# One graph layer on one core: gate logits out of the node products, expert weights asked for earlier, one-hot tiles scaled on ScalarE

## The chip, the core and the metric

The kernel runs on one core of a Trainium2 chip. The metric is the device time of one execution in microseconds, as the median of several runs. A core has five engines that run their own instruction lists: TensorE (matrix products, PE in the profile, with its weight loads as PEld), VectorE (DVE), ScalarE (ACT), GpSimd (POOL) and SyncE (SP), which here only issues DMAs. They wait for each other through semaphores (`wait_ge`, `then_inc`). All instructions of this kernel are written by hand in order, engine by engine; nothing is planned or reordered later.

## The reference

```python
xn = _layernorm(x)                                   # 3125 nodes, 256 features
gate = sigmoid(silu(rbf @ W1 + b1) @ W2 + b2)        # 50000 edges
aggr = segment_sum(gate * xn[src], dst)
x = x + xn + (silu(concat[xn, aggr] @ U1 + c1) @ U2 + c2) + mix(xn)
# mix: per head, k and v layer-normed, kv = k^T v / S, then (q kv) @ wo.T + bo
z = _layernorm(x)
logits = z @ gate_w + gate_b                          # 16 experts
top_probs, top_idx = top_k(softmax(logits), 2)        # renormalised to sum 1
x = x + sum over the two experts of p * ((silu(z @ w1[e]) * (z @ w2[e])) @ w3[e])
```

## The kernel before, in words

The nodes lie in 25 tiles of 128 rows (`NT`), two tiles to an iteration `v` of the node loop (13 iterations, `NB`). The kernel has four stages.

*Setup.* For each tile t, VectorE makes the normed rows, TensorE transposes them and projects them to k and v (`project`), and nine tiles later adds their k^T v sum (`sum_kv`, KLAG = 9). ScalarE copies and squares, VectorE sums the squares (`sum_sq`), makes the scales in batches (`kv_seed`, `kv_step`) and scales k (`scale_k`). SP stores the normed rows tile by tile and loads two parameters behind each store. Behind it the k^T v matrix is folded with `wo` and `wq` into one 256x256 matrix M (`mix_kv`, `mix_a1`, `mix_m`), between the first edge groups.

*Edges.* 98 groups of 512 edges: two products with silu and tanh, gathered source rows multiplied in, and a product with a one-hot matrix that sums messages into windows of `agg`.

*Nodes.* In iteration v TensorE runs `node_u1(v+1)` (24 products of 256 columns), `node_m(v+1)` (12 products, xn with M) and `node_silu(v)` (12 products, silu output with U2), the last two into the same PSUM bank. Operands are split in a high and a low half, so each logical product is three. VectorE adds the bank to x (`x1`), takes statistics, and at the ends of `CHUNKS` makes `rstd` and `nmr`. ScalarE writes the normed rows (`xn2`), SP stores them to `xn2_d`. For the gate logits TensorE transposes the normed rows (`transpose_xn2`, L1509), ScalarE copies them (`copy_xt2`, L807), TensorE multiplies by `gw` (`gate_logits`, L1682) and ScalarE copies the logits (`copy_lg`, L811); `XN2AT` says in which iteration a tile's rows are made. The last five tiles are done behind the loop.

*Routing and experts.* VectorE picks the top two experts (`top`, `top2`), counts them per expert (`count`, with two triangular-sum products on TensorE), turns counts into ranks (`picked`, `ranks`) and, when the count of all tiles is known, into places. The table slot -> node is a product of one-hot matrices: `low_marks(c)` makes one-hots over 128 positions, `high_marks(c)` one-hots over 80 blocks of 128 slots, once times the tile number and once times the row code; four batches (`TCUT`), two of these three factors on VectorE and the row one on ScalarE (the last batch wholly on VectorE). `place(c)` multiplies on TensorE. VectorE reads the table (L1423 to L1425), GpSimd gathers the slot rows together with their two gate weights (`gather_slots`), for which `wts` has been written by one DMA into two extra columns of `xn2_d` (L456). SP loads each expert block's weights (`load_w`), whose expert number it reads from `texp`; that is made behind the last marks (L1413 to L1418). Then comes the expert loop with blocks of 256 slots: `turn` (transposes), `expert_up`, `expert_down`, and GpSimd's scatter with accumulation to the output.

Each queue keeps its order: SP's is xn2 stores, output stores, the `wts` store, then all expert weights; GpSimd's first gather waits for the xn2 stores, for the `wts` store, for the table (`s_tabi`) and for `s_wsl`.

Of the kernel before, what the change touches and what calls it, by code (L numbers as in the profile page):

```python
# [23 lines left out]
i32 = mybir.dt.int32  # L24
# [4 lines left out]
P = 128  # L29
# [16 lines left out]
HC = HF // P  # L46
SB = 256
CHUNKS = ((0, 6), (6, 12), (12, 16), (16, 20), (20, NT))
NB = -(-NT // 2)
XN2AT = {3: (0, 2), 4: (2, 4), 5: (4, 6), 6: (6, 8), 7: (8, 10), 8: (10, 12), 9: (12, 14), 10: (14, 18), 11: (18, 20)}  # L50
RCUT = (0, 6, 12, NT)
XN2B = 4
TCUT = (0, 6, 12, 18, NT)
NTC = len(TCUT) - 1
TAILB = (6, 7, 0, 1)
RBANK = (2, 3, 4)
# [49 lines left out]
def gps_layer(nc, x_d, src_d, dst_d, first_d, rbf_d, W1_d, b1_d, W2_d, b2_d, U1_d, c1_d, U2_d, c2_d,  # L106
              wq_d, wkvT_d, woT_d, bo_d, kg_d, kb_d, vg_d, vb_d, gw_d, gb_d, w1_d, w2_d, w3_d, out_d):
# [6 lines left out]
    with ctx:  # L114
# [22 lines left out]
        U2 = sb("U2", [P, DC, D])  # L137
# [20 lines left out]
        M = wkv[:, :, 0:D]  # L158

# [3 lines left out]
        def part(mem, at, *shape):  # L163
# [4 lines left out]
            if len(shape) == 3:  # L168
# [19 lines left out]
        UMs = [part(fr, 8704 + 1024 * k, 2 * DC, D) for k in range(2)]  # L188
        xns = [[part(fr, 512 * (2 * i + k), DC, 2 * P) for k in range(2)] for i in range(2)]
        ags = [[part(fr, 2048 + 512 * (2 * i + k), DC, 2 * P) for k in range(2)] for i in range(2)]  # L190
        sts = [[part(fr, (4096, 10752)[i] + 512 * k, DC, 2 * P) for k in range(2)] for i in range(2)]
# [22 lines left out]
        xt2 = [oflat[i % 2][:, i // 2 * D:(i // 2 + 1) * D].rearrange("p (c q) -> p c q", c=DC) for i in range(4)]  # L214
# [15 lines left out]
        me, cu = ([part(big, EV + 2000 + 448 * k + NX * (a + r), NX, b - a + 1)  # L230
                   for r, (a, b) in enumerate(zip(RCUT, RCUT[1:]))] for k in range(2))
        mask = [part(big, EV + 2896 + 112 * min(r, 1) * 1, NX, b - a + 1)
                for r, (a, b) in enumerate(((0, 6), (12, NT)))]
        t_a = part(big, EV + 3232, 8, NX)
        tcmp = part(big, EV + 3360, CAPB, NX)
# [14 lines left out]
              for (mem, at), a, b in zip(((flat3(U1), 0), (flat3(h1f), 0), (flat3(wkv), 0), (big, EV + 4608)),  # L250
                                         TCUT, TCUT[1:])]
        tE = [marks(mem, at, (b - a) * NS).rearrange("p (n w) -> p n w", w=NS)
              for (mem, at), a, b in zip(((rbf[0], 0), (rbf[1], 0), (big, EV + 5728)), TCUT, TCUT[1:])]
        c_i = sb("c_i", [P, NX], i32)
        texp = sb("texp", [P, CAPB], i32)
        lastp = sb("lastp", [P, 1], i32)
# [83 lines left out]
        s_tp2 = sem("xn2_transposed")  # L340
        s_xt2 = sem("xt2_copied")
        s_lg = sem("logits_done")
        s_lgc = sem("logits_copied")
# [39 lines left out]
        NPAR = 21  # L383
# [3 lines left out]
        def _(sp):  # L387
# [4 lines left out]
            for k, (a, b) in enumerate(zip(XCUT, XCUT[1:])):  # L392
# [10 lines left out]
                (U2[:, :, :], U2_d.rearrange("(c p) n -> p c n", p=P)),  # L403
# [9 lines left out]
                (gw[:, :, :], gw_d.rearrange("(c p) n -> p c n", p=P)), (gb[:, :], row(gb_d, NX)),  # L413
# [41 lines left out]
            sp.wait_ge(s_wt, 1)  # L455
            sp.dma_start(xn2_d[:, D:XW].rearrange("(t p) k -> p t k", p=P), wts).then_inc(s_wst, 16)  # L456
# [15 lines left out]
            load_w(1, 1, True)  # L472
            end = last_pair(sp, lastp)
# [13 lines left out]
        def _(pool):  # L487
# [92 lines left out]
            pool.wait_ge(s_src, 16)  # L580

# [85 lines left out]
            pool.wait_ge(s_texp, 1)  # L667
# [18 lines left out]
        def _(act):  # L686
# [44 lines left out]
            def edges(n0, h0):  # L731
# [30 lines left out]
                def pair_cast(j):  # L762
                    pair(j)
                    if type(n0) is int and 6 <= j < 9:
                        act.wait_ge(s_mv, 3)
# [37 lines left out]
            def copy_xt2(t, i, bank):  # L803
                act.wait_ge(s_tp2, t + 3)
                if i < 2:
                    act.wait_ge(s_lg, NT - 2 if t == NT - 1 else t + 1)
# [21 lines left out]
            for v in range(NB):  # L828
# [4 lines left out]
                for t in late:  # L833
                    copy_lg(t, 6 + t % 2)
# [1007 lines left out]
```

## Time and profile before

| | us |
|---|---|
| median of 3 runs (lowest, highest) | 1117.7 (1116.98, 1118.97) |
| the profiled execution's time | 1119.88 |
| its span, first to last instruction | 1118.1 |
| PE busy | 1034.4 (93%) |
| DVE busy | 890.0 (80%) |
| ACT busy | 686.4 (61%) |
| POOL busy | 747.4 (67%) |
| mean granted TensorE clock | 0.961 of full speed |

All times in the text that come from the profile count from the start of the span. The stages lie at about 0 to 106 us (setup), 106 to 664 (edges), 664 to 755 (nodes), 755 to 812 (routing) and 812 to the end (experts). Rows of the timeline merge instructions of one line: start, time taken, engine, line, operation, output and inputs with their sizes, count, and in brackets the idle time ahead and what ended it.

### The profile page before, as it was taken

The numbers are of one execution on the slowest core, as the hardware profiler recorded it, in microseconds if no ns is written. First come the engines' busy times: TensorE is split into PE (matmuls) and PEld (weight loads), VectorE is DVE, ScalarE is ACT, GpSimd is POOL, SyncE is SP. The second block draws the span as 40 slices with busy tenths as digits, with TensorE's granted clock in tenths as the row PEclk, the third lists the DMA queues.
The fourth block names the chain that finished last, engine by engine and source line by source line (L and its number), as shares of the span: only waits on it lengthen the run. The fifth ranks groups of instructions, "written<-read, shape, count | busy, mean of one in ns | idle before, by whom it ended". The sixth has DMA issues, their size and how long they took to land.

```text
span 1118.1 us, 23447 instructions
## 1 busy us (share of the span) xinstructions
PE 1034.4 (93%) x7884; PEld 978.7 (88%) x7884; DVE 890.0 (80%) x1411; ACT 686.4 (61%) x1055; POOL 747.4 (67%) x703
## 2 busy tenths in 40 slices
PE   4897999999999999999999999994299999999995
PEld 2465899999999999999999989994199999999995
DVE  7877888888999888888888863388677777777773
ACT  2562667766666666666666635663066677777663
POOL 5447777777777777777777746530147777777765
PEclk9998999999999999999999999995599999999998
DMA  8211454455544454454545411221468888988972
GB/s 242 78 53 44 138 142 143 142 143 142 143 142 142 143 142 142 141 142 142 143 142 142 133 37 39 75 78 44 117 200 227 223 220 226 231 224 216 239 193 22
DMA packets 118495, 159.74 MB, mean 143 GB/s; under 512 B 20536, under 2 KB 91020, under 8 KB 118412
## 3 DMA queue, kind: packets, MB, share of 16 engines
q0 software_dynamic: 31104, 66.28, 25.8%
q1 hardware_dynamic: 86748, 91.60, 25.4%
q8 instruction: 48, 0.79, 0.3%
q10 hardware_dynamic: 560, 0.79, 0.2%
q14 instruction: 35, 0.29, 0.1%
HBM read 142.42 MB, written 18.17 MB: 144 GB/s over the span
## 4 chain that ended last, share of the span: by engine, by line
PE 85%; DVE 9%; issue 2%; DMA 2%; ACT 1%; DVEq 0%; POOL 0%; POOLq 0%; SPq 0%; ACTq 0%
PE ps L1588 25%; PE ps L1769 16%; PE ps L1599 15%; PE ps L1542 8%; PE ps L1781 8%; PE ps L1643 3%; PE ps L1516 2%; PE ps L1655 2%; PE ps L1668 2%; PE ps L1756 1%; PE ps L1682 1%; DVE st L974 1%; PE ps L1525 1%; DMA hgx<-xn_rows,hgx 1%; PE ps L1526 1%
## 5 line engine op out<-in xcount | busy, mean ns | idle before, releaser
L1588 PE MATMUL ps<-fr 128*128 128x256 f32 x2352 | 307.8, 287 | 3.4 <-DVE fr L1036 3.4
L1588 PEld LDWEIGHTS ps<-fr 128*128 128x128 f32 x2352 | 290.1, 193 | 4.3 <-DVE fr L1036 4.2
L589 POOL DMA_INDIRECT big<-xn_rows,srcs x200 | 218.8, 1094 | 61.3 <-issue 61.3
L589 POOL DMA_INDIRECT hgx<-xn_rows,srcs x192 | 210.1, 1094 | 58.5 <-issue 58.5
L741 ACT ACTIVATE h1f<-ps,b 128x512 f32<-128x512 f32 x196 | 124.2, 684 | 168.5 <-PE ps L1542 167.6
L1599 PEld LDWEIGHTS ps<-oh,big 128*128 128x128 f32 x1568 | 190.7, 192 | 8.8 <-DVE big L1172 0.5
L1769 PE MATMUL ps<-fr 128*128 128x256 f32 x1536 | 191.7, 285 | 2.7 <-issue 1.4
L1769 PEld LDWEIGHTS ps<-fr 128*128 128x128 f32 x1536 | 188.4, 194 | 3.3 <-issue 1.8
L1599 PE MATMUL ps<-oh,big 128*128 128x96 f32 x1568 | 189.0, 274 | 0.4 <-DVE big L1181 0.4
L1036 DVE TENSOR_TENSOR fr<-h1f,fr 128x1024 fp32r<-128x1024 f32 x98 | 120.0, 1225 | 52.4 <-ACT fr L744 52.4
L661 POOL DMA_INDIRECT out<-xnT,idx x64 | 119.0, 1860 | 49.2 <-issue 34.4
L1440 DVE TENSOR_TENSOR fr<-big,fr 128x1024 fp32r<-128x1024 f32 x96 | 117.6, 1225 | 21.9 <-ACT fr L876 21.7
L876 ACT CAST fr<-big 128x1024 fp32r<-128x1024 f32 x95 | 99.7, 1049 | 50.6 <-PE ps L1781 35.8
L1158 DVE TENSOR_TENSOR big<-ps,b2bc 128x1024 f32<-128x1024 f32 x98 | 119.3, 1217 | 1.3 <-PE ps L1588 1.0
L1542 PE MATMUL ps<-fr 128*128 128x512 f32 x392 | 108.6, 399 | 1.9 <-DVE fr L1031 1.9
L748 ACT ACTIVATE big<-big 128x1024 f32<-128x1024 f32 x98 | 103.6, 1057 | 8.6 <-DVE big L1158 8.5
L744 ACT CAST fr<-h1f 128x1024 fp32r<-128x1024 f32 x98 | 102.6, 1047 | 8.5
L1781 PE MATMUL ps<-fr 128*128 128x256 f32 x768 | 99.8, 286 | 0.4 <-DVE fr L1462 0.4
L1781 PEld LDWEIGHTS ps<-fr 128*128 128x128 f32 x768 | 94.0, 192 | 0.8 <-DVE fr L1462 0.7
L647 POOL DMA_INDIRECT hgx<-xn_rows,idx x56 | 59.9, 1070 | 32.0 <-POOL idx L643 22.9
L1542 PEld LDWEIGHTS ps<-fr 128*128 128x128 f32 x392 | 68.1, 191 | 11.1 <-DVE fr L1031 2.1
L1031 DVE TENSOR_TENSOR fr<-rbf,fr 64x512 fp32r<-64x512 f32 x98 | 68.3, 698 | 3.1 <-DVE big L1133 0.2
(216 smaller groups left out, 1378.7 us busy)
## 6 DMA issues: line engine op xcount, KB each, us to landing
big<-in_w SPq DMA_DIRECT2D x128, 256.0 KB, 4.3
rbf<-in_rbf SPq DMA_DIRECT2D x98, 256.0 KB, 3.0
big<-in_w SPq DMA_DIRECT2D x32, 512.0 KB, 4.4
xn_rows<-xn SPq DMA_DIRECT2D x26, 128.0 KB, 2.5
big<-xn_rows,srcs POOLq DMA_INDIRECT x200, 3.2
xn_rows<-hgx SPq DMA_DIRECT2D x24, 128.0 KB, 2.4
hgx<-xn_rows,srcs POOLq DMA_INDIRECT x192, 3.3
x_nodes<-in_x SPq DMA_DIRECT2D x2, 768.0 KB, 9.6
```

Of the source, the lines that this page charges most:

```text
L589: pool.indirect_dma_start(hg[i % HB][:, s, :], None, xn_d[:, :], bass.IndirectOffsetOnAxis(srcs[:, col:col + 1], 0))\
L661: pool.indirect_dma_start(out_d[:, :], bass.IndirectOffsetOnAxis(idx[p][:, 2 + s:3 + s], 0), ys[p][:, s, :], None, bounds_check=N - 1, oob ...
L741: act.activation(h1f[:, m, :], ps[:, m, :], ACT.Silu, bias=b1[:, m:m + 1]).then_inc(s_silu, 1)
L748: act.activation(th[p], th[p], ACT.Tanh, scale=0.5).then_inc(s_th, 1)
L1036: dve.tensor_tensor(h1s[p][1], h1f[:, :, :], h1s[p][0].bitcast(f32), ALU.subtract).then_inc(s_hlo, 1)
L1158: dve.tensor_tensor(th[p].rearrange("p (b s) d -> p b (s d)", b=2), ps[:, 2 + 4 * p:4 + 4 * p, :], b2bc[:, :, :].rearrange("p s d -> p (s ...
L1440: dve.tensor_tensor(halves[1], wst[r][p], halves[0].bitcast(f32), ALU.subtract).then_inc(s_wlo[r], 1)
L1542: last = mm(ps[:, m, :], W1s[k][:, m * P:(m + 1) * P], rbs[p], start=k == 0, stop=k == 1)
L1588: last = mm(ps[:, 2 + 4 * p + s // 2, (s % 2) * D:(s % 2 + 1) * D], h1s[p][a][:, c, s * P:(s + 1) * P], W2s[b][:, c, :], start=c == 0 and ...
L1599: last = mm(ps[:, 4 + p, c * w_n:(c + 1) * w_n], msg[p][:, s, c * P:(c + 1) * P], oh[p][:, s, 0:w_n], start=s == 0, stop=s == ET - 1)
L1769: last = mm(ps[:, 2 * m + q, k * SB:(k + 1) * SB], ws[q][a][:, 2 * m + c, k * P:(k + 1) * P], xTs[p][b][:, c, :], start=c == 0 and (a, b) ...
L1781: last = mm(ps[:, 4 + p, s * D:(s + 1) * D], hids[p][a][:, k, s * P:(s + 1) * P], ws[r][b][:, k, :], start=k == 0 and (a, b) == PARTS[0], ...
```

## The change

Three things are done together.

1. The logits are no longer computed from the stored normed rows. With g the centred gate matrix, LN(x1) g = rstd (x1 g). x1 is a sum of the node's own scaled row and of products with M and U2, so M and U2 get 32 more columns (256 to 288, `DG`): 16 for U2 g (and for M g), 16 for xn g alone, which is multiplied by the row's standard deviation (`std1`) in `x1`. The small matrices are made in setup (`centre_gate`, `keep_gate`, products at t = 19 and t = 23), in `mix_a1` and behind edge group 5. The transposes, copies and products of the old way go. The chunks of statistics, counts and tops are cut anew and come some iterations earlier.
2. The first two blocks' expert numbers are made as soon as the counts are known (`experts(0, 2)`), and SP loads their weights before it stores `wts`. The rest of the expert numbers follows behind the table.
3. In three of four batches ScalarE multiplies the high marks by the tile number, tile by tile; batches 2 and 3 have 8 and 5 tiles. The weights `wts` are made behind all marks.

```diff
-CHUNKS = ((0, 6), (6, 12), (12, 16), (16, 20), (20, NT))
+DG = D + 2 * NX
+CHUNKS = ((0, 6), (6, 12), (12, 20), (20, NT))
-RCUT = (0, 6, 12, NT)
+RCUT = (0, 12, 20, NT)
-TCUT = (0, 6, 12, 18, NT)
+TCUT = (0, 6, 12, 20, NT)
...
 sp: for t in range(NT):
+                if t == 2:
+                    for dst, src in ((gw[:, :, :], gw_d), (woL, wo_d), (U2L, U2T_d)):
+                        sp.dma_start(dst, src.rearrange("(c p) n -> p c n", p=P)).then_inc(s_gp, 16)
+                    sp.dma_start(cbT[:, :, :], cbT_d).then_inc(s_gp, 16)
...
-            sp.wait_ge(s_wt, 1)
-            sp.dma_start(xn2_d[:, D:XW].rearrange("(t p) k -> p t k", p=P), wts).then_inc(s_wst, 16)
             sp.wait_ge(s_texp, 1)
             load_w(0, 0, True)
             load_w(1, 1, True)
+            sp.wait_ge(s_wt, 1)
+            sp.dma_start(xn2_d[:, D:XW].rearrange("(t p) k -> p t k", p=P), wts).then_inc(s_wst, 16)
+            sp.wait_ge(s_texp, 2)
...
 pool, before the edge gathers:
+            pool.wait_ge(s_gt, 2)
...
 act, routing:
-            for c in range(NTC - 1):
+            for c in range(NTC):
                 act.wait_ge(s_eq, c + 1)
+                if c < NTC - 1:
+                    for i in range(TCUT[c + 1] - TCUT[c]):
+                        act.activation(tB[c][:, 2 * i:2 * i + 2, 0, :], tE[c][:, 2 * i:2 * i + 2, :], ACT.Copy,
+                                       scale=float(TCUT[c] + i))
...
 dve, setup:
+            def centre_gate():
+                dve.wait_ge(s_gt, 1)
+                link(gw = gw - column mean); link(cbT sum); link(gcb = gw * cbT)
+                dve.sem_inc(s_gc, 1)
+                dve.memset(U2[:, :, D + NX:DG], 0.0)
+                dve.scalar_tensor_tensor(std1[:, :], mv[:, :, 1], EPS, rstd[:, :], ALU.add, ALU.mult)
+            def keep_gate():
+                dve.wait_ge(s_gt, 2)
+                three copies out of PSUM: U2 g, wo g, cg
+                dve.sem_inc(s_gc, 1)
+                if t == NT - 1:
+                    centre_gate()
+                if t == NT + 2:
+                    keep_gate()
...
 dve, x1(v, q, n):
+                link(dve.tensor_tensor(lg[:, t, :], of[:, :, D + NX:DG], std1 ..., ALU.mult))
+                dve.tensor_tensor(x[:, t, :], of[:, :, 0:D], x[:, t, :], ALU.add)
+                dve.tensor_tensor(lg[:, t, :], of[:, :, D:D + NX], lg[:, t, :], ALU.add).then_inc(s_x1, 1)
...
 dve, node loop:
+                if v == 3: top(0, 6, 0)
+                if v == 4: top(0, 6, 1)
+                if v == 6: top(6, 12, 0)
+                if v == 7: top(6, 12, 1)
+                if v == 8: count(0)
+                if v == 9: ranks(0)      (picked(0) right behind x1)
+                if v == 10: top(12, 20, 0)
+                if v == 11: top(12, 20, 1); count(1)
-            top2(12, 20)
-            picked(1)
-            ranks(1)
-            low_marks(1)
             top2(20, NT)
             count(2)
             link(dve.tensor_tensor(exw[:, :], tops[:, 1, :], tops[:, 0, :], ALU.subtract))
             dve.sem_inc(s_dif, 1)
+            low_marks(0)
             (wait for the counts; c_e, cend, off)
+            experts(0, 2)
             places(0, 12)
             high_marks(0)
             high_marks(1)
-            picked(2)
-            ranks(2)
-            low_marks(2)
+            low_marks(1)
+            for r in (1, 2):
+                picked(r)
+                ranks(r)
             places(12, NT)
             high_marks(2)
+            low_marks(2)
+            high_marks(3)
+            low_marks(3)
+            dve.sem_inc(s_wsl, 2)
             (wait for exp; three operations that make wts; s_wt)
-            low_marks(3)
-            high_marks(3)
-            (expert numbers of all blocks, last pair)
             (wait for the table, read it; s_tabi; slot tables)
+            (last pair)
+            experts(2, CAPB)
...
 pe, setup:
+                if t == 19:
+                    pe.wait_ge(s_flag, 1); pe.wait_ge(s_gp, 64)
+                    2 products ones x gw, then_inc(s_gt, 1)
+                if t == 23:
+                    pe.wait_ge(s_gc, 1)
+                    4 products U2L x gw, 4 products woL x gw, 2 products ones x gcb, then_inc(s_gt, 1)
 pe, mix_a1: + pe.wait_ge(s_gc, 2), 2 products kvt x g1
 pe, edge group 5: + pe.wait_ge(s_mv, 3), 4 products wq x gcb into the group's bank
 pe, node_m and node_silu:
-                            last = mm(ps[:, 2 + 2 * q + h, 0:D], ...
+                            last = mm(ps[:, 2 + 2 * q + h, 0:DG], ...
-                if v == 10:
+                if v == 9:
                     last = count(0)
 (all transpose_xn2 and gate_logits calls go)
```

## Rows read from the trace of the kernel before

**Rows 1.** Windows of 20 us: busy time of each engine, granted clock, DMA share, GB/s.
```profile
780.00:800.00 20.00, 6.66 (x47) 5.46 (x44) 18.16 (x38) 2.56 (x4) 0.00 (x0) 0.50 0.08 2
```
**Rows 2.** Timeline of TensorE in the node loop.
```profile
677.50 3.04 PE L1643 MATMUL ps<-fr 128*128 128x256 f32 x24
...
683.26 3.04 PE L1643 MATMUL ps<-fr 128*128 128x256 f32 x24
...
736.30 0.96 PE L1682 MATMUL ps<-gw,oh 128*128 128x16 f32 x8
```
**Rows 3.** Timeline of TensorE in an edge group.
```profile
647.61 1.09 PE L1542 MATMUL ps<-fr 128*128 128x512 f32 x4
...
648.54 1.92 PE L1599 MATMUL ps<-oh,big 128*128 128x96 f32 x16
```
**Rows 4.** Timeline of setup around t = 23 to 26.
```profile
83.87 0.42 DVE L1022 TENSOR_TENSOR oh<-big,kvr 128x256 f32<-128x256 f32 x1
...
84.33 1.88 PE L1516 MATMUL ps<-wkv,xnT 128*128 128x512 f32 x4
...
87.36 0.69 DVE L991 TENSOR_REDUCE ssq<-h1f 128x8 f32<-128x512 f32 x1 [0.27 <-ACT h1f L705]
```
**Rows 5.** Timeline of VectorE from the last iterations to the counts.
```profile
750.45 0.69 DVE L1241 TENSOR_TENSOR x_nodes<-ps,x_nodes 128x512 f32<-128x512 f32 x1 [0.67 <-PE ps L1668]
...
754.84 0.41 DVE L1241 TENSOR_TENSOR x_nodes<-ps,x_nodes 128x256 f32<-128x256 f32 x1
...
755.29 0.43 DVE L974 BATCH_NORM_STATS2 st<-x_nodes 128x6 f32<-128x256 f32 x1
...
758.65 0.17 DVE L1334 SCALAR_TENSOR_TENSOR big<-mv,rstd 128x5 f32<-128x5 f32 x1
...
767.13 0.24 DVE L1250 TENSOR_TENSOR big<-big,gb 128x80 f32<-128x80 f32 x1 [0.93 <-ACT big L811]
...
770.70 0.51 DVE L1272 TENSOR_TENSOR big<-big 128x208 f32<-128x208 f32 x1
```
**Rows 6.** Timeline of places and marks, VectorE and ScalarE.
```profile
774.23 0.17 DVE L1361 TENSOR_SCALAR c_i<-ps 128x16 int32<-128x16 f32 x1 [1.80 <-PE ps L1727]
...
776.69 1.16 DVE L1387 TENSOR_TENSOR rbf<-iota,big 128x960 bf16<-128x960 f32 x1
777.94 1.28 ACT L867 ACTIVATE U<-rbf,row_of 128x480 bf16<-128x480 bf16 x2 [3.68 <-DVEq L1394]
777.99 1.16 DVE L1395 TENSOR_TENSOR U<-rbf,tile_of 128x960 bf16<-128x960 bf16 x1
...
783.43 1.83 DVE L1309 TENSOR_TENSOR xnT<-iota,big 128x768 bf16<-128x768 f32 x2
```
**Rows 7.** Timeline from the weights' store to the table.
```profile
790.65 0.37 SPq L456 DMA_DIRECT2D xn_rows<-hgx  x1
...
796.26 2.02 PE L1739 MATMUL ps<-big,xnT 128*128 128x160 bf16 x14 [4.49 <-DVE big L1395]
...
798.32 0.24 DVE L1423 TENSOR_SCALAR big<-ps 128x80 int32<-128x80 f32 x1
```
**Rows 8.** Timeline from the first gather to the first expert product.
```profile
801.05 0.96 POOL L647 DMA_INDIRECT hgx<-xn_rows,hgx  x1 [51.38 <-DVEq L1432]
...
809.55 1.09 PE L1756 MATMUL ps<-ident,hgx 128*128 128x128 f32 x4 [11.27 <-DMA hgx<-xn_rows,hgx]
...
812.09 4.78 PE L1769 MATMUL ps<-fr 128*128 128x256 f32 x24 [1.45 <-issue]
```
**Rows 9.** DMA issues (KB each, us to landing), gathers of L647, a window.
```profile
big<-in_w SPq DMA_DIRECT2D x128, 256.0 KB, 4.3
...
xn_rows<-hgx SPq DMA_DIRECT2D x1, 25.0 KB, 6.2
...
DMA to landing us min/median/max: 3.9/4.8/7.5
...
793.50:794.00 0.50, 0.00 (x0) 0.00 (x0) 0.50 (x1) 0.00 (x0) 0.00 (x0) 0.50 0.10 1
```

More of the change, by code:

```diff
@@ L158, in gps_layer @@
         M = wkv[:, :, 0:D]
+        MG = wkv[:, :, 0:DG]
+        gcb, g1 = (v_a[:, 64 + 32 * i:96 + 32 * i].rearrange("p (c n) -> p c n", c=DC) for i in range(2))
+        cg = v_b[:, 64:64 + NX]
+        std1 = v_c[:, 64:64 + NT]
+        cbT = v_c[:, 96:96 + 2 * DC].rearrange("p (c n) -> p c n", c=DC)
         big = sb("big", [P, NT * 2 * D])
@@ L213, in gps_layer @@
         oflat = [oh[i][:, :, :].rearrange("p s w -> p (s w)") for i in range(2)]
-        xt2 = [oflat[i % 2][:, i // 2 * D:(i // 2 + 1) * D].rearrange("p (c q) -> p c q", c=DC) for i in range(4)]
+        woL, U2L = (part(hgx, 1024 * i, DC, D) for i in range(2))
         khs = [oflat[i][:, 0:2 * (P + 2)].rearrange("p (j c) -> p j c", j=2) for i in range(2)]
@@ L229, in gps_layer @@
         t_b = part(big, EV + 1200, NT, 2, NX)
[L230 to L235, printed above, removed]
+        me, cu, mask = ([part(big, EV + 2000 + 448 * k + NX * (a + r), NX, b - a + 1)
+                         for r, (a, b) in enumerate(zip(RCUT, RCUT[1:]))] for k in range(3))
+        t_a = part(big, EV + 3344, 8, NX)
+        tcmp = part(big, EV + 1200, CAPB, NX)
         tops = part(big, EV + 4000, 2, NT)
@@ L1278, in count @@
                 flat = lambda ap: ap.rearrange("p a b -> p (a b)")
[L1279 removed]
+                link(dve.tensor_tensor_scan(flat(cu[r]), flat(mask[r]), flat(me[r]), 0.0, ALU.mult, ALU.add))
                 dve.sem_inc(s_m12, 1)
@@ L1365, in _, with experts @@
             link(dve.tensor_tensor(off, cend, c_e, ALU.subtract))
+            def experts(a, b):
+                shape = [P, b - a, NX]
+                link(dve.tensor_tensor(tcmp[:, a:b, :], cend.unsqueeze(1).to_broadcast(shape),
+                                       iota[:, a:b].unsqueeze(2).to_broadcast(shape), ALU.is_le))
+                link(dve.tensor_reduce(texp_f[:, a:b], tcmp[:, a:b, :], X, ALU.add))
+                link(dve.tensor_scalar(texp[:, a:b], texp_f[:, a:b], float(NX - 1), None, ALU.min))
+                dve.sem_inc(s_texp, 1)
             def places(a, b):
@@ L1567, in mix_a1 @@
                 for c in range(DC):
-                    last = mm(ps[:, 4, c * D:(c + 1) * D], kvt[:, c, :], woT[:, c, :], start=True, stop=True)
+                    mm(ps[:, 4, c * D:(c + 1) * D], kvt[:, c, :], woT[:, c, :], start=True, stop=True)
+                pe.wait_ge(s_gc, 2)
+                for c in range(DC):
+                    last = mm(ps[:, 7, 112 + c * NX:112 + (c + 1) * NX], kvt[:, c, :], g1[:, c, :], start=True, stop=True)
                 last.then_inc(s_mx, 1)
@@ L1600, in scatter @@
                                       oh[p][:, s, 0:w_n], start=s == 0, stop=s == ET - 1)
+                    if type(i) is int and i == 5:
+                        pe.wait_ge(s_mv, 3)
+                        for m in range(DC):
+                            for c in range(DC):
+                                last = mm(ps[:, 4 + p, 480 + m * NX:480 + (m + 1) * NX], wq[:, c, m * P:(m + 1) * P],
+                                          gcb[:, c, :], start=c == 0, stop=c == DC - 1)
                     last.then_inc(s_sc, 1)
```

232 lines of the change are left out of this document (100 added, 132 removed).

## The prediction, made before the changed kernel was run

> **What bounds the kernel now.** I read the view by windows first: from 780 to 800 us TensorE works 6.66 of 20 us at a granted clock of 0.50 (the 1.2 GHz level), and VectorE 18.16 of 20 [rows 1]. That stretch, from the end of the node loop to the first expert product, belongs to VectorE and to what waits for its chain. Ahead of it the timeline of TensorE shows the node loop without holes: an iteration takes 5.76 us (677.50 to 683.26) while no gate work is in it, and at 736.30, with it, the loop is 6.96 us behind that pace [rows 2]. So the loop is TensorE's, and removed products there count in full. Then I followed the timeline through the routing stretch: last `x1` at 754.84, first high marks at 776.69, table read at 798.32, first gather at 801.05, first expert product at 812.09 [rows 5 to 8].
>
> **Setup.** The added pieces lie where every step counts. At t=19 two small products, 0.10 us each (eight of the same kind take 0.81 to 0.96 us) [rows 2]: +0.2. At t=23 TensorE waits for `centre_gate`, which VectorE reaches only behind `scale_k(15)`, done at 84.29; its three operations up to the signal take 0.65 us (0.19 and a link each), so the signal is there at 84.95 to 85.1. TensorE would go on at 84.3 to 84.5 [rows 4]: 0.6 us of waiting, with project(24) queued behind it, and behind that the square, `sum_sq(24)` at 87.36 and the serial `kv` chain. Then ten small products, 1.0 us. `keep_gate` puts three operations into this chain, +0.65. `mix_a1` gets two products at the low clock and one copy, +0.4; edge group 5 four products, +0.4, and on VectorE two small operations. Four more DMA issues on SP at t=2 (about 0.5 us each) stand ahead of the stores of tiles 2 to 4, whose buffers are asked for only some 5 us later: nothing. Pool's new wait is for an event before 90 us and it starts gathering after it: nothing. Sum +3.3 us; bounds +1.5 (the products vanish in waits) and +5 (the stall doubled at the low clock).
>
> **Node loop.** Up to the end of `node_silu(9)` the gate work costs: that end is 736.30; eight iterations from 677.50 at 5.76 and one more would make it 729.34, so 6.96 us go [rows 2]. Added columns: the 512-column product of the same type takes (648.54 - 647.61)/4 = 0.233 us [rows 3], the 256-column one 5.76/48 = 0.120; slope 0.44 ns a column, 14 ns for 32. Until there are 21 x 12 = 252 such products: +3.5 us; bounds 0 (they stay at 0.120, a weight load hides them; but 16-column products come every 0.10 us with weight loads of the same shape, so at 256 the columns decide) and 28 (each at the 512-column price, 0.233). 288 lies next to 256, so I take the line between them. `count(0)` comes one iteration earlier: +0.65. So `x1(9)` starts near 733.5 instead of 736.3.
> The Trainium skill, page "TensorE: Matmul & The Clock Gate", section "Back-to-back issue gap", gives a sustained stream 81 ns at 128 and 131 ns at 512 columns; by that the 32 columns would cost an estimated 4 ns, 1.0 us here. The trace does not agree: 233 ns at 512.
> From `x1(9)` on VectorE is the later one. Per operation of the 8-tile `top` I take 0.325 us with its link (between the 80- and 208-column rows 767.13 and 770.70) [rows 5]. v=9: `x1` with two logit operations 1.27, `picked(0)` 0.73, statistics 0.78, moments 0.75, 13 links 2.6, `ranks(0)` 1.2 = 7.3. v=10: 1.27 + 0.8 + 8 operations 2.6 = 4.7. v=11: 1.27 + 0.8 + 6 operations 1.95 + `count(1)` 1.2, and the last `x1` 0.9 = 6.1. Together 18.1: the last `x1` ends at 751.6, before 755.25 [rows 5]: -3.65. TensorE would be ready a microsecond earlier, so it isn't late next. In the loop's earlier iterations VectorE needs under 5 us of 6.1, ScalarE loses its copies: nothing.
>
> **Routing stretch, from the end of the last `x1`.** Before: 755.25 to 777.85 (end of the first marks, call it T) = 22.6 us [rows 5, 6]. After: statistics to `nmr` 3.57 (755.29 to 758.82, unchanged), no wait for transposes, copies and logits; 15 operations of `top2` at 0.275 (767.13 to 770.70 has 13) 4.15+0.1; `count(2)` on 5 tiles in place of 13, 1.05; the difference and `low_marks(0)` 2.1, which cover the count products; carry to `off` 1.05; `experts(0, 2)` three operations 0.75; `places` 1.40 and marks 1.16 [rows 5, 6]. Sum 15.3: -7.3.
> After T the three tile multiplications (1.16 each) go to ScalarE, but `low_marks(1)`, formerly hidden, and a bigger share of ranks come in. With 1.83 for a 6-tile low mark, 1.16 for a high one [rows 6]: marks(1) to 1.25, low(1) 3.2, ranks 6.3, `places(12, NT)` 8.1, marks(2) 9.6, low(2) 12.1, marks(3) and multiplication 14.2, low(3) 15.8, weights 16.6 (all after T). ScalarE: a batch of six is six 160-element operations near 0.29 plus the 1.28 of rows; the third batch ends at 13.7. That 0.29 is an estimate from the 0.64 that one of 480 elements takes; at 0.64 each the batch would end at 16.5 and the table be kept at T+21.2, still ahead of what follows [rows 6]. TensorE's last 26 products at 0.147 (798.32 - 796.26 over 14) give the table at T+17.7, `tabi` at T+18.4 [rows 7]. Before, the table was read at T+20.5.
> Now the weights' store. Before it was issued at 790.65, 7.7 us ahead of the table; now `weights` stands behind all marks, issue at T+16.6, and the landing that the profile gives is 6.2 us [rows 7, 9]: T+22.9. Pool waits for it before its first gather and starts 0.8 us later, T+23.7; before it was T+23.2 [rows 8]. So the shorter table buys nothing: the store takes the wait. Queued behind Pool's wait are all four gathers, and TensorE's first transpose waits for them.
> Cover lost or kept: `experts(2, CAPB)` and `w_low(0)` end near T+24, before `slots_low` needs VectorE.
>
> **Weights early.** SP issues ten loads from T-2.6 on; it was idle there. Ten issues of 0.4 to 0.5 us, slowed by the queue to some 7 us, and 4.3 us to land (8 at worst) put the 3 MB down by about T+12, ahead of the store [rows 9]. Before, gathers and loads met: from the first gather's issue to the first transpose 809.55 - 801.05 = 8.5 us [rows 8]. On quiet queues I take 1.27 + 3.9, the shortest landing of such a gather [rows 9], 5.2 us: -3.3. Bounds: 8.5 (no gain) and 4.5. From there to the first product 2.54 us as before, and its 24 products run at the low clock as before, 4.6 us [rows 8]; the expert loop behind is TensorE's own.
>
> **Sum.** +3.3 - 3.65 - 7.3 + 0.5 - 3.3 = -10.5 us. The profiled execution has a span of 1118.1 and a time of 1119.88 us; it lay 2.2 above the median of 1117.7, and the difference is put on the median: 1107.2 us.
>
> **Rivals.** (a) The store does not hold the gather. The packets of the 25 KB store end by about 793.7, 3.1 us after issue [rows 9]; if rows are down then, or the landing is shorter in the new place, the gather goes at T+20.5, or at T+19.2 by the table: 3.2 to 4.5 us earlier, 1103.4. For it: the packets; against it: the landing of 6.2. [...]
> (b) The gather is as slow as before (8.5 us, its latency not the loads') or setup costs 5 us: 2 to 3.3 us less gained, 1110.
> (c) Slower: a product past 256 columns pays the 512-column price, 0.233 us. The loop has 25 x 12 = 300, so 300 x (0.233 - 0.134) = 30 us more than forecast, 1137. It decides from 0.134 + 10.5/300 = 0.169 us per product. For it: the trace shows no shape between; against it: 0.233 is no more than the line through both shapes with a fixed part of 7 ns, as if each column had its own price [rows 2, 3].
> (d) No change: the node loop's gain and the routing's are eaten by VectorE (operations in the loop and setup): needs 8 us that I do not see.
>
> **Numbers.** Forecast 0.58, (a) 0.20, (b) 0.15, (c) 0.03, (d) 0.04. Own range of the forecast 1104.5 to 1109.5. Low end: (a) with columns partly hidden, 1101; high end: (b) with two more microseconds of VectorE, 1112. A difference of 0.2%, 2.2 us, is about what measurements tell from none. Faster 0.93, same 0.03, slower 0.04.
>
> **What would show it.** Node products start every 0.134 us; iterations near 6.1 us and no transposes; last `x1` about 0.4 us earlier than before in absolute time (setup +3.3), first edge stage products 3 us later. From the first marks to the first gather some 23.7 us, and Pool's wait ended by the DMA of the weights and not by the table; gather to first transpose near 5 us. First expert product near 801.6. Wrong if the gather follows the table at once, if a product over 0.15 us is found, or if the edge stage starts over 5 us later.

## The result, and the profile after

The changed kernel takes 1114.4 us (median of 20 runs, 1110.5 to 1118.6) against 1117.7 for the kernel before (20 runs, 1115.7 to 1119.4): a ratio of 0.9970, 95% interval 0.9959 to 0.9981. In a second comparison, the run again1 below, it took 1112.6 against 1117.4, ratio 0.9963 (0.9949 to 0.9976). It is faster, by 3.4 and 4.8 us; the forecast was 10.5, and both medians lie above its range of 1104.5 to 1109.5.

The profiled execution of the changed kernel took 1111.8 us, 2.6 below its median, and that of before 1119.9, 2.2 above its own. So the two traces, 8.1 us apart, show more gain than the medians. I compare them stage by stage first; what that difference is made of stands behind the experiments.

TensorE at t=23 of the setup, and the first gates (timeline; start, duration, what, idle time before and its releaser):
```profile
86.86 1.96 PE L1589 MATMUL ps<-gw,hgx 128*128 128x16 f32 x16 [0.44 <-DVEq L1056]
88.66 0.60 PE L1592 MATMUL ps<-v_a,ones 128*128 128x16 f32 x4
...
111.46 4.63 PE L1633 MATMUL ps<-fr 128*128 128x256 f32 x24 [2.79 <-DVE fr L1016]
```
The ten products are twenty instructions: the trace has two of 0.11 us for each fp32 product. They and the wait of 0.44 us keep project(24) back by 2.7 us, from 86.42 to 89.11.

In the node loop, first one of the two groups of 288 columns (`node_m`), then TensorE's waits in it:
```profile
L1706 PE MATMUL ps<-fr 128*128 128x288 f32 x150 | 22.6, 299 | 4.8 <-DVE big L1260 3.2 <-DVEq L1247 1.7
```
```profile
701.64 1.86 PE L1706 MATMUL ps<-fr 128*128 128x288 f32 x12 [0.58 <-DVE big L1260]
708.59 1.86 PE L1706 MATMUL ps<-fr 128*128 128x288 f32 x12 [0.62 <-DVE big L1260]
722.01 1.86 PE L1706 MATMUL ps<-fr 128*128 128x288 f32 x12 [1.02 <-DVE big L1260]
728.98 1.86 PE L1706 MATMUL ps<-fr 128*128 128x288 f32 x12 [0.63 <-DVE big L1260]
748.38 1.06 PE L1706 MATMUL ps<-fr 128*128 128x288 f32 x6 [0.31 <-DVE big L1260]
```
Twelve of these products start over 1.60 us, 0.133 each, and an iteration without a wait takes 6.07 us (679.83 to 685.90), against 5.76 [rows 2] and, with gate work, 7.06 before (701.78 to 708.84). But five times `node_m` waits for `x1` (L1260 is its last operation), 3.2 us in all, which before it never did. Why VectorE was late is seen a few lines up the timeline. VectorE, then GpSimd, ahead of the first of those waits:
```profile
696.43 0.17 DVE L941 TENSOR_TENSOR v_a<-rstd 128x6 f32<-128x6 f32 x1
696.63 1.29 DVE L942 SCALAR_TENSOR_TENSOR v_b<-v_a,v_c 128x6 f32<-128x6 f32 x1
697.96 1.21 DVE L943 SCALAR_TENSOR_TENSOR rstd<-v_b,rstd 128x6 f32<-128x6 f32 x1
699.20 1.22 DVE L1354 SCALAR_TENSOR_TENSOR big<-mv,rstd 128x6 f32<-128x6 f32 x1
700.58 0.19 DVE L1257 TENSOR_TENSOR big<-ps,v_c 128x32 f32<-128x32 f32 x1 [0.16 <-DVE big L1354]
```
```profile
696.61 1.29 POOL L527 TENSOR_TENSOR fr<-h1f,fr 128x512 fp32r<-128x512 f32 x1 [2.27 <-ACT fr L808]
697.86 1.28 POOL L527 TENSOR_TENSOR fr<-xnT,fr 128x512 fp32r<-128x512 f32 x1
699.10 1.29 POOL L527 TENSOR_TENSOR fr<-big,fr 128x512 fp32r<-128x512 f32 x1
```
An operation on six elements takes 0.17 us, and 1.2 to 1.3 when it starts just behind a GpSimd subtraction: it ends when that one ends, and the next falls behind the next. `x1` (L1257), which reads PSUM, isn't slowed, but it starts 2.3 us late: its bank was ready at 698.2.

The routing stretch: last `x1`, first marks, the weights' store on SyncE, the table, and from the first gather to the first expert product:
```profile
757.75 0.16 DVE L1260 TENSOR_TENSOR big<-ps,big 128x16 f32<-128x16 f32 x1
...
772.11 2.46 DVE L1417 TENSOR_TENSOR rbf<-iota,big 128x960 bf16<-128x960 f32 x2
...
776.86 0.59 SPq L473 DMA_DIRECT2D big<-in_w  x1
789.74 0.37 SPq L478 DMA_DIRECT2D xn_rows<-hgx  x1
...
790.61 0.24 DVE L1447 TENSOR_SCALAR big<-ps 128x80 int32<-128x80 f32 x1 [0.95 <-PE ps L1756]
...
796.43 0.96 POOL L655 DMA_INDIRECT hgx<-xn_rows,hgx  x1 [46.40 <-issue]
...
800.96 1.09 PE L1773 MATMUL ps<-ident,hgx 128*128 128x128 f32 x4 [10.39 <-DMA hgx<-xn_rows,hgx]
...
803.50 5.12 PE L1786 MATMUL ps<-fr 128*128 128x256 f32 x24 [1.45 <-issue]
```
The chain that ended last names what held the gather (start, duration, what):
```profile
789.74 5.53 DMA xn_rows<-hgx
795.27 0.02 issue
...
796.43 0.31 POOL hgx L655
...
797.70 3.17 DMA hgx<-xn_rows,hgx
...
800.96 1.09 PE ps L1773 x4
```
It does not pass through the table, read at 790.61; it passes through the store of the pair weights. With T = 773.3, the end of the first marks, the table is at T+17.3 and the gather at T+23.1; before they were at T+20.5 and T+23.2 [rows 6 to 8].

Stage by stage, in us, read from the timelines of these two and of the experiments in whose stay the kernel before took 1117 us (a stay is a time on the chip in which several kernels run beside each other). "First gates" is the start of the first products with W2 (L1633 in the changed kernel), "last scatter" the end of the last product with a one-hot matrix that sums messages (L1644):

| kernel | to first gates | edges, to last scatter | to last `x1` | to first expert product | rest |
|---|---|---|---|---|---|
| before | 106.5 | 557.6 | 91.1 | 56.8 | 306.0 |
| changed | 111.5 | 556.1 | 90.3 | 45.7 | 306.4 |
| again1 (changed) | 109.8 | 556.1 | 90.4 | 45.6 | 306.5 |
| small_low_after | 109.6 | 557.6 | 86.6 | 45.5 | 305.7 |
| store_early | 110.4 | 557.7 | 92.3 | 41.9 | 306.4 |
| setup_late | 106.9 | 557.1 | 90.3 | 45.6 | 306.7 |
| both | 107.0 | 557.5 | 92.0 | 41.9 | 306.6 |
| spread | 107.2 | 556.1 | 86.4 | 42.4 | 306.4 |
| experts_early (on before) | 106.3 | 554.7 | 91.3 | 53.6 | 305.7 |
| small_low_before | 106.5 | 555.0 | 91.3 | 56.8 | 305.8 |

The node loop must be compared at the same clock. TensorE has waited some 2 us for it, and in some executions it starts it at 1.2 GHz. The first twelve products of the loop in before, before1 (a second profile of it, below), the changed kernel and store_early:
```profile
665.97 2.90 PE L1655 MATMUL ps<-fr 128*128 128x256 f32 x12 [1.87 <-issue]
760.60 1.66 PE L1655 MATMUL ps<-fr 128*128 128x256 f32 x12 [1.99 <-issue]
669.23 1.82 PE L1706 MATMUL ps<-fr 128*128 128x288 f32 x12 [1.69 <-DVEq L1247]
670.18 3.14 PE L1706 MATMUL ps<-fr 128*128 128x288 f32 x12 [2.12 <-DVEq L1247]
```
The granted clock from 664 to 672 us is 0.79 in before and 1.00 in the changed kernel. Where the start is slow, the kernel before takes 91.1 to 91.3 and the changed one 92.0 and 92.3 (both, store_early); where it is at full clock, 89.9 (before1, the only such trace of that kernel, from a later stay) and 90.3 to 90.4. So at equal clock the change made the loop 0.4 to 1.2 us longer, and the 0.8 us that the pair of profiles shows as gain is the clock.

### The profile page after: what moved, and what is told of

Read it like the earlier page. It is cut to its first block, busy times and chain, and to the rows that moved or that the text cites. A ratio compares the mean times of both kernels' runs of the same rounds, so it can differ in the third digit from the quotient of the medians.

```text
span 1109.9 us, 23181 instructions
## 1 busy us (share of the span) xinstructions
PE 1021.1 (92%) x7770; PEld 964.7 (87%) x7770; DVE 899.2 (81%) x1443; ACT 680.4 (61%) x1027; POOL 747.2 (67%) x703
## 4 chain that ended last, share of the span: by engine, by line
PE 81%; DVE 11%; issue 2%; DMA 2%; ACT 1%; SPq 1%; POOLq 0%; POOL 0%; DVEq 0%; ACTq 0%
PE ps L1633 25%; PE ps L1786 16%; PE ps L1644 15%; PE ps L1798 8%; PE ps L1568 8%; PE ps L1542 2%; PE ps L1694 1%; PE ps L1773 1%; DMA xn_rows<-hgx 1%; PE ps L1706 1%; DVE st L954 1%; PE ps L1551 1%; PE ps L1719 1%; PE ps L1552 1%; DVE xnT L1329 1%
## 5 line engine op out<-in xcount | busy, mean ns | idle before, releaser
L1633 PE MATMUL ps<-fr 128*128 128x256 f32 x2352 | 306.9, 287 | 3.3 <-DVE fr L1016 3.3
L1633 PEld LDWEIGHTS ps<-fr 128*128 128x128 f32 x2352 | 289.4, 192 | 4.2 <-DVE fr L1016 4.1
L597 POOL DMA_INDIRECT big<-xn_rows,srcs x200 | 221.3, 1106 | 61.3 <-issue 61.3
L1644 PEld LDWEIGHTS ps<-oh,big 128*128 128x128 f32 x1568 | 189.8, 192 | 8.6 <-DVE big L1177 0.5
L1644 PE MATMUL ps<-oh,big 128*128 128x96 f32 x1568 | 188.2, 273 | 0.4 <-DVE big L1186 0.4
L1466 DVE TENSOR_TENSOR fr<-big,fr 128x1024 fp32r<-128x1024 f32 x96 | 117.6, 1225 | 18.3 <-ACT fr L856 17.7
```

Of the source, the lines that this page charges most:

```text
L597: pool.indirect_dma_start(hg[i % HB][:, s, :], None, xn_d[:, :], bass.IndirectOffsetOnAxis(srcs[:, col:col + 1], 0))\
L1466: dve.tensor_tensor(halves[1], wst[r][p], halves[0].bitcast(f32), ALU.subtract).then_inc(s_wlo[r], 1)
L1633: last = mm(ps[:, 2 + 4 * p + s // 2, (s % 2) * D:(s % 2 + 1) * D], h1s[p][a][:, c, s * P:(s + 1) * P], W2s[b][:, c, :], start=c == 0 and ...
L1644: last = mm(ps[:, 4 + p, c * w_n:(c + 1) * w_n], msg[p][:, s, c * P:(c + 1) * P], oh[p][:, s, 0:w_n], start=s == 0, stop=s == ET - 1)
```

## The experiments

**The collisions of VectorE and GpSimd.** GpSimd's subtraction in the node loop is cut to two columns, in the changed kernel (small_low_after) and in the one before (small_low_before), after one full pass that fills the buffers (the kernel leaves out most of the low halves, so it serves for timing alone):
```
-return pool.tensor_tensor(halves[1], of, halves[0].bitcast(f32), ALU.subtract)
+return pool.tensor_tensor(halves[1][:, :, 0:2], of[:, :, 0:2],
+                          halves[0].bitcast(f32)[:, :, 0:2], ALU.subtract)
```


> The changed kernel with GpSimd's subtractions in the node loop (the low halves of the node operands) cut to 2 columns of each row: leaves out nearly all of GpSimd's work there, TensorE's products stay. Theory A (VectorE's two-input operations that start beside a GpSimd subtraction last until it ends, 0.5 to 1.3 us instead of 0.17 to 0.26, and that makes x1 late, for which node_m then waited 0.3 to 1.0 us in five iterations): these operations fall to 0.17 to 0.26 us, no iteration waits for x1, each takes 6.1 us, the last x1 ends 3 to 4 us earlier. Rival B (VectorE has too many operations by themselves, whatever GpSimd does): TensorE still waits for x1 in the same iterations, under 1 us gained.

It took 1107.1 us, 5.5 less than again1 beside it; ratio to before 0.9912 (0.9897 to 0.9926). VectorE's two-input operations by form in the changed kernel, 664 to 758 us (count, busy us, mean ns, idle before):
```profile
L1275 DVE TENSOR_TENSOR big<-big 128x96 f32<-128x96 f32 x4 | 4.8, 1207 | 0.1
L1279 DVE TENSOR_TENSOR big<-big,v_a 128x96 f32<-128x96 f32 x4 | 4.0, 997 | 0.1
L942 DVE SCALAR_TENSOR_TENSOR v_b<-v_a,v_c 128x6 f32<-128x6 f32 x6 | 3.2, 528 | 0.2
...
L1278 DVE TENSOR_REDUCE v_a<-big 128x6 f32<-128x96 f32 x4 | 1.0, 254 | 0.1
```
The same (4 lines further down in the code), and the 288-column products, without GpSimd's work:
```profile
L946 DVE SCALAR_TENSOR_TENSOR v_b<-v_a,v_c 128x6 f32<-128x6 f32 x6 | 1.0, 173 | 0.2
L1279 DVE TENSOR_TENSOR big<-big 128x96 f32<-128x96 f32 x4 | 1.0, 258 | 0.1
L1283 DVE TENSOR_TENSOR big<-big,v_a 128x96 f32<-128x96 f32 x4 | 1.0, 258 | 0.1
```
```profile
L1710 PE MATMUL ps<-fr 128*128 128x288 f32 x150 | 23.4, 307 | 1.9 <-DVEq L1251 1.9
```
1207 and 997 ns become 258, 528 becomes 173; the reduction, with one input, was at 254 all along. No product waits for `x1`, and the loop takes 86.6 us. It started at 1.2 GHz (its first twelve products last 3.10 us), so it stands against 92.0 and 92.3: 5.4 to 5.7 us less, as the medians say. Theory A holds, with more gain than its 3 to 4 us.

> The kernel before with GpSimd's subtractions in the node loop cut to 2 columns of each row: leaves out nearly all of GpSimd's work there. Theory A (the kernel before had little to lose by the collisions, since its loop ran 0.5 us longer per iteration and its VectorE had fewer operations): under 1.5 us faster than before, where the same edit took 5.5 us off the changed kernel. Rival B (the collisions cost both the same): 4 to 6 us faster.

It took 1117.7 us, as before beside it: ratio 0.9996 (0.9984 to 1.0008). The collisions are in the trace of before too, and cost nothing there: its iterations with gate work take 7.06 us, and from 672 to 755 us VectorE is busy for 46.6 us, against 58.6 in the changed kernel. So it was the change that made them count: it shortened the iteration to 6.07 us, put two more operations into `x1` and moved more of the tops and counts into the loop. Which of these weighs most isn't separated.

**The order of VectorE's operations** (spread, on top of the two edits below). In the first and second batch of statistics the last Newton round, the scaling and ScalarE's rows are put off by one iteration:
```
+if v in (3, 6):                      # behind x1(v) and its statistics
+    newton(rstd[...], ..., 1)
+    link(dve.scalar_tensor_tensor(nmr[...], mv[...], -1.0, rstd[...], ALU.mult, ALU.mult))
+    dve.sem_inc(s_rs, 1)
-XN2AT = {3: (0, 3), 4: (3, 6), 6: (6, 9), 7: (9, 12), 10: (12, 16), 11: (16, 20)}
+XN2AT = {4: (0, 3), 5: (3, 6), 7: (6, 9), 8: (9, 12), 10: (12, 16), 11: (16, 20)}
```


> The same as both, and VectorE's order in the node loop changed: behind the first and second batch of statistics the third Newton round and the scaling of the means (4 operations) are put off to behind the next x1, and ScalarE's normalized rows with them by one iteration. Theory A (VectorE is late only because the last three or four of these operations start while GpSimd subtracts and last until it ends; put off, they run in the 2.5 us of each iteration in which GpSimd waits): the waits of TensorE for x1 at the fourth and fifth, and at the seventh and eighth iteration (0.6, 0.6, 1.0, 0.6 us) go, the wait at the last (0.3) stays, -2.5 to -2.9 us against both. Rival B (other operations take their place beside GpSimd's): the waits move to other iterations, under 1 us.

1101.5 us, ratio to before 0.9861 (0.9847 to 0.9876), and 4.0 less than both. TensorE's waits in its node loop:
```profile
L1717 PE MATMUL ps<-fr 128*128 128x288 f32 x150 | 22.2, 296 | 2.0 <-DVEq L1249 1.7 <-DVE big L1262 0.3
```
Of 3.2 us of waiting for `x1`, 0.3 is left, as expected; the loop takes 86.4, 3.9 less than the 90.3 of the loops that also began at full clock. (In the trace of both it took 92.0; its first twelve products last 3.22 us at the low clock, here 1.83.) Theory A, with more gain than expected. Nothing of the computation is left out: this is the fastest kernel of the study.

**The store of the pair weights** (store_early):
```
 high_marks(1)
 low_marks(1)
+dve.wait_ge(s_ex, 1)
+... the three operations that make wts, moved here from behind low_marks(3)
+dve.sem_inc(s_wt, 1)
```


> The changed kernel with the pair weights (sum, reciprocal, product) made right behind the second low marks instead of behind the last, so that their store is issued some 8 us earlier. Theory A (the gather is held by the landing of that store, which ended 4.2 us behind the table in the changed kernel's trace): the first gather follows the token table by about 0.5 us; the three small operations, 0.8 us, now lie ahead of the third batch of marks; in all -3.4 us against the changed kernel (-2.6 to -4.2), ratio to before near 0.994. Rival B (the gather is held by something else, the stores of the node rows or GpSimd's own queue): no change, or +0.8.

1108.4 us, 4.2 less than again1 beside it; ratio 0.9914 (0.9899 to 0.9928). Store, table and gather:
```profile
780.42 1.13 SPq L478 DMA_DIRECT2D xn_rows<-hgx  x1
793.67 0.24 DVE L1447 TENSOR_SCALAR big<-ps 128x80 int32<-128x80 f32 x1 [1.28 <-PE ps L1756]
...
795.57 0.96 POOL L655 DMA_INDIRECT hgx<-xn_rows,hgx  x1 [43.03 <-issue]
```
From the table to the gather 1.9 us instead of 5.8, where 0.5 had been expected, and the chain that ended last now runs through the table's operations. Theory A, at the upper end of its gain.

**The setup** (setup_late; products_late without the first edit; loads_late with it alone):
```
-if t == 2:                  # SyncE: four added loads
+if t == 12:
-if t == 19: / if t == 23:   # TensorE: added products
+if t == 21: / behind the first sum_kv that follows the projections
-if t == NT - 1: centre_gate()    if t == NT + 2: keep_gate()
+if t == NT: centre_gate()        keep_gate() ahead of the first h1_low
```


> The changed kernel with its setup moved out of the projection loop: SyncE's four added loads at t=12 instead of t=2, the two centring products at t=21, the ten gate products behind the projection loop (behind the first product pair that follows project(24), where TensorE had waited 3.0 us for VectorE), the centring of the gate at VectorE's t=25, the three copies of its results ahead of the first h1_low, where VectorE had waited 3.2 us. Theory A (these products, VectorE's copies and the loads are what makes the first gates 4.9 us later than before): the first gates start at 107 to 108 us instead of 111.5, and the kernel is 2.5 to 4 us faster than the changed one. Rival B (the edges' start is held by something that moves with the clock or with the indirect gathers, and the edges give back what they get): under 1 us.

1109.2 us, 3.4 less than again1; ratio 0.9932 (0.9920 to 0.9945). The first gates start at 106.9. Theory A. TensorE there:
```profile
84.35 1.88 PE L1541 MATMUL ps<-wkv,xnT 128*128 128x512 f32 x4
88.14 1.85 PE L1594 MATMUL ps<-gw,hgx 128*128 128x16 f32 x16
89.85 0.60 PE L1597 MATMUL ps<-v_a,ones 128*128 128x16 f32 x4
...
106.93 3.14 PE L1632 MATMUL ps<-fr 128*128 128x256 f32 x24 [2.71 <-DVE fr L1016]
```
project(24) starts at 84.35, as before the change [rows 4], and the products fall into TensorE's wait behind it.

> The changed kernel with the added products, the centring and the three copies late as in setup_late, and SyncE's four loads at t=2 as in the change. Theory A (products and copies cost 2.5 to 3.5 us of the 4.9, the loads the rest): 2 to 2.5 us faster than the changed kernel, 1 to 1.4 us slower than setup_late's 3.4. Rival B (the products carry it all): 3.4 us, as setup_late.

> The changed kernel with SyncE's four added loads at t=12 instead of t=2, nothing else. Theory A (the loads hold up the stores of the normalized rows and by them the buffers, 1.4 us by t=19): the projection of tile 19 starts 1.4 us earlier and the kernel is 1 to 1.5 us faster than the changed one. Rival B (the pause comes back elsewhere ahead of the edges, the products at t=19 and t=23 carry it all): under 0.4 us, and the setup moved as a whole (3.4 us) owes its gain to the products.

These ran in later stays on the chip, in which every kernel, the one before too, took 1184 to 1228 us, so the whole times say little: products_late 1197.8 against 1206.9 (ratio 0.997, 0.992 to 1.002), with the changed kernel beside it in a later comparison 1204.3 against 1203.6; loads_late 1198.4 against 1204.5 (0.995, 0.991 to 0.999) and once more 1.003 (0.997 to 1.010). Their traces up to the first gates can be read: with the products late these start at 106.7 and 107.4, with the loads alone late at 109.5 and 111.7, and the unchanged setup had 109.6 to 112.8. The products and copies carry the setup's cost, the loads none of it that can be seen: rival B in both. In whole time it isn't shown.

The spread of these starts has a pattern. Eleven traces have the products in the projection loop. In five of them (again2, again4, again5, again6, loads_late2) the granted clock from 88 to 92 us is 0.50 to 0.71, under project(24), and the first gates start at 111.3 to 112.8; in the other six it is 1.00 there, and they start at 109.5 to 111.5. The nine without the products there start at 106.3 to 107.4, also where the clock falls to 0.73 and 0.75 (small_low_before, before1). So the setup of the changed kernel costs some 3 us ahead of the first gates, and up to 6 where the clock falls there. That the clock is the cause is argued from these rows; no run changes it alone.

> The changed kernel with the added products, the centring and the three copies late, and SyncE's four loads at t=2 as in the change, beside the changed kernel. In the look so far its first gates started at 106.7 us, as early as with the loads late too (106.9), and those of the kernel with the loads alone late at 109.5 and 111.7, as in the changed one. Theory B (the products and copies carry all of the setup's cost, the loads nothing): 3 to 4 us faster than the changed kernel. Theory A (the loads have a share): 2 to 2.5 us.

That comparison is the one with the changed kernel above: no difference in whole time at a spread of 20 us, so neither theory, although its first gates start 4.2 us earlier than those of the changed kernel beside it (107.4, 111.6).

**Both** edits:

> The changed kernel with the pair weights made early and the setup moved out of the projection loop. Theory A (the two are separate costs, one ahead of the edges, one behind the routing): the gains add, -4.2 and -3.4 against the changed kernel, so near 1105 us, ratio to before 0.989. Rival B (a gain at the start is given back by the indirect gathers or the clock): under 2 us better than the pair weights early alone, 1108.4.

1105.4 us, ratio 0.9889 (0.9874 to 0.9903), 12.3 below the kernel before beside it. again1 was 4.8 below its own, so the two edits gave 7.5, where 4.2 and 3.4 make 7.6: they add.

**The weights early alone** (experts_early, on the kernel before):
```
+experts(0, 2)          # ahead of places(0, 12)
-sp: wait s_wt, store wts; wait s_texp; load_w(0), load_w(1)
+sp: wait s_texp; load_w(0), load_w(1); wait s_wt, store wts
```


> The kernel before with one edit of the change alone: the experts of the first two blocks made ahead of the marks, and SyncE's six loads of them ahead of the store of the pair weights. Theory A (behind the token table the end waits for these loads: 8.5 us from first gather to first transpose, 4.5 in the changed kernel): first gather 2.2 us behind the table as before or up to 2 us later, where the store comes to hold it; first transpose 4.5 us behind the gather; the three operations of the first blocks 0.7 us ahead of the marks; in all -2 to -3.3 us. Rival B (the gathers themselves take 8 us behind a store of many small packets): no gain.

1114.1 us against 1117.7, ratio 0.9976 (0.9965 to 0.9986): 3.6 of gain.
```profile
798.23 1.52 POOL L648 DMA_INDIRECT hgx<-xn_rows,hgx  x1 [51.49 <-DVEq L1439]
...
803.45 1.08 PE L1763 MATMUL ps<-ident,hgx 128*128 128x128 f32 x4 [8.04 <-DMA hgx<-xn_rows,hgx]
```
From gather to transpose 5.2 us instead of 8.5 [rows 8], the prediction's number (4.5 was expected here); the gather follows the table by 2.7 us, as before. Theory A, slightly above its range.

**How far executions of one kernel differ** (again1, again2, before1).

> The changed kernel once more, beside the kernel before in the same stay on the chip. Its 20 runs lay at 1110.5 to 1118.6 and bunched near 1112, 1115 and 1118, those of before at 1115.7 to 1119.4; the two profiled executions differ by 8.1 us, the medians by 3.4. Theory A (the profiled pair flatters the change; its executions differ among themselves by how long TensorE is held at 1.2 GHz, since in the 20 runs the mean granted clock falls from 0.970 at 1110.5 to 0.961 at 1118.6): again a ratio near 0.997, and this profile, where it is not again one near 1112, is longer in the stretches in which its granted clock is lower. Rival B (the executions differ by when GpSimd's and VectorE's instructions collide in the node loop, 660 to 758 us): the same ratio, but the time is gained or lost between 660 and 758 us, at full clock.

Its profile was again a short one, 1110.2 us, so it can't tell between the two theories.

> The changed kernel, one more look, for where an execution above 1114 us loses its time. In ten profiles so far the way from the first gates to the last scatter took 554.7 to 557.7 us and that from there to the last x1 of the changed kernel 90.3 to 92.3, by how long TensorE ran at 1.2 GHz behind the pause ahead of each. Theory A (these stretches and no others carry the spread): an execution near 1117 has more of both, at a granted clock near 0.50 for longer between 84 and 136 us and between 664 and 672 us, or in the projections. Rival B: it loses the time in the experts' loop, 306 us in each profile so far.

> The kernel before, one more look. Theory A (the profiled execution on which the forecast's terms rest, 1119.9, was long in the edges, 557.6 us from first gates to last scatter, where the two profiles of kernels that are the same up to there took 554.7 and 555.0): near 555 us, last scatter near 661.5, span near 1115.5. Rival B (557.6 is usual for it): last scatter near 664.

These took 1216.6 and 1213.6 us, and four further profiles of the changed kernel (again3 to again6) 1189 to 1203. They belong to the same later stays, in which something adds time to the edges: 632 to 657 us in the changed kernel, 651.9 in the one before, where the table has 554.7 to 557.7. In again6 TensorE is idle at issue for 36 of the 89.5 added us (23.1 at L1633 and 12.9 at L1644). What the cause is, and whether it is the chip, stays open: one of these stays has the chip number on which the kernel before took 1117.7 us earlier. So the theories on the edges can't be judged there. The other stages can: the experts' loop and what follows take 305.7 to 306.9 us in every trace, which speaks against rival B of again2, and again2 had late first gates (112.8), as theory A has it.

No execution of the changed kernel above 1112 us was profiled in the first stays. What the ten profiles there show is that stages of equal code differ with the granted clock: the edges of the code before take 554.7 us where it is 1.00 from 112 to 136 us, and 557.6 where it is 0.91. experts_early, then the kernel before (busy us by engine, granted clock, DMA share, GB/s):
```profile
112.00:136.00 24.00, 21.61 (x155) 19.77 (x154) 21.27 (x26) 18.06 (x24) 19.12 (x17) 1.00 0.48 135
```
```profile
112.00:136.00 24.00, 21.62 (x135) 19.29 (x133) 19.92 (x24) 15.94 (x22) 19.08 (x17) 0.91 0.47 135
```
The changed kernel has 556.1 at 1.00 (spread), 1.1 to 1.4 more than the code before at that clock. In its 26 runs the mean granted clock falls as the time rises, from 0.970 at 1110.5 us to 0.961 at 1118.6. That speaks for theory A of again1; it isn't shown for the executions above 1112.

## Why the prediction was wrong

The step that failed is the node loop's gain of 3.65 us. The setup was priced too low, and the time of one profiled execution was carried over to the median.

**Node loop, -3.65: wrong, and this is the term that failed.** The columns were right (0.133 us against 0.134, rival (c) out), and so was the iteration (6.1). What failed is the sentence "In the loop's earlier iterations VectorE needs under 5 us of 6.1, ScalarE loses its copies: nothing". It summed durations of VectorE's operations as if each ran alone; beside GpSimd a 6-element one takes up to seven times that. Measured: -0.8 in the pair, and 0.4 to 1.2 us more than before at equal clock, so the term missed by 4 to 5 us. Without the collisions the loop takes 86.6, 4.5 to 4.7 less than before from the same slow start, even 0.9 more than forecast. The rows for it were in the trace of before, where operations of this kind average 340 to 830 ns (128x96: 513 to 832; 128x6: 337 and 691); I took the short ones.
The Trainium skill says it: "SBUF — State Buffer", section "SBUF: two separate sides": a VectorE operation with two SBUF inputs and a GpSimd operation that reads SBUF exclude each other, and the one that starts first keeps the shared ports for the whole instruction. The traces agree: the slowed ones have two SBUF inputs (1.29 us instead of 0.17), they end with GpSimd's, and the ones with a PSUM operand or one input are at their 0.19 and 0.25 us.

**Setup, +3.3: too low.** Of the 3.3 us the prediction had 0.8 behind the first gates (`mix_a1` and edge group 5), so 2.5 ahead of them. Measured: first gates 3.1 to 3.9 us later in three of the four traces of the first stays and 4.9 in the changed kernel's own profile; its project(24) starts 2.0 us later than again1's (87.14), and TensorE's granted clock was 0.73 from 28 to 32 us, where again1 has 1.00. In the later stays it was 3 to 6 us (109.6 to 112.8 against 106.7). The edges add 1.1 to 1.4 us at full clock, for the 0.8. Moving the pieces gave 3.4 back. Two of its numbers were off: the ten products took 2.3 us, not 1.0, since each is two instructions (the row of eight that the price came from holds four products), and the three copies added nothing (from `sum_sq(24)` to the last `scale_k` 13.7 us before, 13.8 after), where 0.65 had been put. SyncE's loads cost nothing, as said.

**The sum was put on the median.** Forecast: 10.5 us off 1119.9, a profiled time of 1109.4. Measured: 1111.8, so the terms missed by 2.4 in the pair of traces. That small miss is luck: the pair compares a loop at full clock with one at 1.2 GHz, and edges of 556.1 with a long 557.6, which kernels with the same code up to there passed in 554.7 and 555.0. The other 4.8 of the 7.2 us are where the two profiled executions stand: I took 2.2 off for the one before, and the changed kernel's lay 2.6 below its median. At equal clock the change is worth +3.1 to +4.9 (first gates), +1.1 to +1.4 (edges), +0.4 to +1.2 (loop), -11.1 (to the first expert product) and +0.4: -6.1 to -3.2, and the medians say -3.4 and -4.8. What makes six of the 26 executions longer than 1116 us stays open.

**Routing, -7.3: right.** Last `x1` to T is 15.4 us, forecast 15.3. Table at T+17.3 (17.7), ScalarE's tile parts 0.245 us each (0.29).

**The store takes the wait, +0.5: right in mechanism.** Gather at T+23.1 (forecast 23.7). Rival (a) is out: the chain goes through the store for 5.5 us, and with the store issued earlier the gather followed the table by 1.9 us instead of 5.8.

**Weights early, -3.3: right,** 4.5 us from gather to transpose (forecast 5.2), and the one edit alone gave 3.6.

Rival (b), 1110, came near by its time. It had either a gather as slow as before, which is out (4.5 us), or a setup of 5 us, which some traces show; the loop that missed most is not in it. Rival (d), no change because VectorE eats the gain in loop and setup, had the loop's mechanism, but for the whole time, and got 0.04.

## What to carry to other kernels

When a change shortens TensorE's iteration, the slack of the other engines goes too: sum their work in the new iteration with the durations that they have beside each other in the trace, not their shortest. Then put small two-input VectorE operations into the part of the iteration in which GpSimd waits; four of them moved by one iteration gave 4.0 us here. A transfer that was issued early enough becomes the wait once the chain beside it is shortened: look at where its issue stands in the new order and move it with the same edit. And before a sum of 10 us is put on a median, compare a second profile of the kernel before: one execution was 3 us off in one stage. Compare stages at the same granted clock: the loop seemed 0.8 us shorter and was up to 1.2 longer.

## What the runs showed of the hardware

- VectorE and GpSimd: a 6-element operation of 0.17 us takes up to 1.29 beside a 512-element GpSimd subtraction, a 96-element one 1.21 on average instead of 0.26.
- fp32 products of 16 columns are two instructions of 0.10 to 0.11 us each (20 for ten products).
- The store of 25 KB in 8-byte pieces held its waiter for 5.5 us behind its issue, the usual 128 KB store has 2.4.
- The same stage differs by where TensorE runs at 1.2 GHz: the loop's first twelve 256-column products take 1.66 or 2.90 us, the edges 554.7 or 557.6.
- The same kernels took 1184 to 1228 us in three later stays and 1117 in the earlier ones, nearly all of it in the edges, in part with TensorE idle at issue between its own products. What differed isn't known.
